# Placing the two operands of the split-precision matmuls 192 bytes apart modulo 512

## What is computed

```python
# layer 0
h = modulate(layernorm(x), shift_msa, scale_msa)
x = x + gate_msa * attention(h)              # 16 heads of 16 features, masked
h = modulate(layernorm(x), shift_mlp, scale_mlp)
x = x + gate_mlp * (gelu(h @ fc1.T + b1) @ fc2.T + b2)      # 256 -> 1024 -> 256
# layer 1
h = layernorm(x) * g + b + shift
q, k, v = split(h @ Wqkv.T)                  # 16 heads of 64 features, q and k normalized
x = x + (softmax(q @ k.T / 8) @ v) @ Wout.T
gate = softmax(x @ Wgate.T)                  # 8 experts, each takes its 1,024 best tokens
y = gelu(layernorm(tokens) @ fc1s[e].T + b1s[e]) @ fc2s[e].T + b2s[e]
x[tokens] += gate_value * y
```

## Time and profile before

| | us |
|---|---|
| median of three runs | 2468.11 |
| the profiled execution | 2465.28 |
| its span, first to last instruction | 2463.5 |
| TensorE busy with matmuls | 2333.9 (95%) |
| TensorE weight loads | 2072.9 (84%) |
| VectorE, ScalarE, GpSimd busy | 1908.8 (77%), 1549.2 (63%), 1030.6 (42%) |
| mean granted TensorE clock | 0.969 |

### The profile page before, as it was taken

One profiled execution on the slowest core, in us unless ns is written; L12 is line 12 of the kernel. 1 busy time (PEld: TensorE's weight loads), 2 busy tenths in 40 slices (PEclk: granted clock), 3 DMA queues, 4 the chain that ended last, 5 costly groups with the idle time before them and its releaser, 6 DMA issues. The chain is left out here.

```text
span 2463.5 us, 67114 instructions
## 1 busy us (share of the span) xinstructions
PE 2333.9 (95%) x24912; PEld 2072.9 (84%) x24912; DVE 1908.8 (77%) x3763; ACT 1549.2 (63%) x2982; POOL 1030.6 (42%) x939
## 2 busy tenths in 40 slices
PE   7999999999999899999999999999999727999997
PEld 6888888899999788888888888888888626999996
DVE  8999999667666688888888888888888586666663
ACT  6999998766666456565555656565555454556553
POOL 5888888200000234444343434344343203454543
PEclk9999999999999899999999999999999856999998
DMA  4111110101101000000000000000000112333422
GB/s 144 44 40 41 43 38 25 55 22 32 30 23 32 27 19 13 17 13 17 13 17 13 17 17 13 17 13 17 13 17 13 59 20 66 96 91 82 98 50 34
DMA packets 78720, 89.21 MB, mean 36 GB/s; under 512 B 18480, under 2 KB 72496, under 8 KB 76080
## 3 DMA queue, kind: packets, MB, share of 16 engines
q1 hardware_dynamic: 66352, 71.10, 9.3%
q0 software_dynamic: 12288, 17.05, 4.2%
HBM read 62.42 MB, written 25.69 MB: 36 GB/s over the span
## 5 line engine op out<-in xcount | busy, mean ns | idle before, releaser
L1275 POOL TENSOR_TENSOR a_rq<-a_vq,minus_half 128x8 f32<-128x8 f32 x256 | 417.4, 1640 | 97.9 <-DVE a_vq L1299 97.9
L1222 ACT ACTIVATE a_sq<-a_bqk 128x512 f32<-128x512 f32 x256 | 152.8, 597 | 351.0 <-PE a_bqk L126 348.5
L1270 POOL TENSOR_TENSOR a_rstd<-a_veps,minus_half 128x1 f32<-128x1 f32 x63 | 34.8, 552 | 580.5 <-DVE a_veps L1346 580.5
L124 PE MATMUL a_bqk<-wqk_hi,a_h_lo 128*128 128x512 f32 x512 | 207.4, 405 | 3.5 <-DVE a_h_lo L1315 3.5
L126 PE MATMUL a_bqk<-wqk_hi,a_h_hi 128*128 128x512 f32 x512 | 201.1, 393 | 0.0
L125 PE MATMUL a_bqk<-wqk_lo,a_h_hi 128*128 128x512 f32 x512 | 201.0, 393 | 0.0
L1291 DVE TENSOR_TENSOR a_qk<-a_bqk,a_rq 128x512 f32<-128x512 f32 x256 | 175.6, 686 | 29.8 <-POOL a_rq L1275 29.7
L2041 DVE TENSOR_TENSOR e_u_lo<-e_u,e_u_hi 128x512 fp32r<-128x512 f32 x128 | 88.8, 694 | 127.3 <-ACT e_u_hi L1904 126.6
L1899 ACT ACTIVATE e_u<-e_bu,e_b 128x512 f32<-128x512 f32 x128 | 88.3, 690 | 157.2 <-PE e_bu L126 155.2
L1207 ACT COPY a_vs<-a_ba 64x512 f32<-64x512 f32 x256 | 148.6, 580 | 53.6 <-PE a_ba L126 48.9
L1283 DVE TENSOR_REDUCE a_ss<-a_sq 128x8 f32<-128x512 f32 x256 | 173.7, 678 | 2.6 <-ACT a_sq L1222 1.0
(11 more groups left out here) (329 smaller groups left out, 8045.6 us busy)
## 6 DMA issues: line engine op xcount, KB each, us to landing
a_qk<-gates_of_rows SPq DMA_DIRECT2D x32, 256.0 KB, 4.3
tokens<-a_xs SPq DMA_DIRECT2D x64, 128.0 KB, 1.7
out<-a_xs SPq DMA_DIRECT2D x64, 128.0 KB, 1.7
e_w<-in_fc1s SPq DMA_DIRECT2D x8, 1024.0 KB, 4.9
e_w<-in_fc2s SPq DMA_DIRECT2D x8, 1024.0 KB, 4.9
a_gate<-gates_of_rows SPq DMA_DIRECT2D x122, 64.0 KB, 2.5
X<-in_x SPq DMA_DIRECT2D x56, 128.0 KB, 2.1
wst<-in_qkv_w SPq DMA_DIRECT2D x16, 128.0 KB, 2.5
```

What stands on the lines that cost most here:

```text
L124: tensor.matmul(to, w_lo, x_hi, start=start, stop=False)
L1222: nc.scalar.activation(sq[:, n * BK:(n + 1) * BK], b_qk[:, n * BK:(n + 1) * BK], ACT.Square).then_inc(s["sq"], 1)
L1275: nc.gpsimd.tensor_tensor(rq[:, 8 * n:8 * n + 8], vq[:, 8 * n:8 * n + 8], g.mhalf[:, 0:8], ALU.pow).then_inc(s["rq"], 1)
```

## The change

No instruction is added, removed or moved. The room of one small area changes, two groups of tensors change their order, and five unused tensors (a bare call of `m.sb`) fill gaps. 

```diff
-        small = m.sb("m0_small", [P, P])
+        small = m.sb("m0_small", [P, 64])          # MlpStart: 512 -> 256 bytes
...
-        st = m.sb("a0_st", [P, 6])                 # attention0_phase: these six tensors
-        veps = m.sb("a0_veps", [P, 1])             # move from ahead of a0_hT
-        mv = [m.sb(f"a0_mv{q}", [P, 2]) for q in range(2)]
-        rstd = [m.sb(f"a0_rstd{q}", [P, 1]) for q in range(2)]
         hT = m.sb("a0_hT", [P, DC, T2])
...
         o_hi, o_lo = (m.sb("a0_o_" + n, [P, DC, P], F32R) for n in ("hi", "lo"))
+        st = m.sb("a0_st", [P, 6])
+        veps = m.sb("a0_veps", [P, 1])
+        mv = [m.sb(f"a0_mv{q}", [P, 2]) for q in range(2)]
+        rstd = [m.sb(f"a0_rstd{q}", [P, 1]) for q in range(2)]
         wp_hi, wp_lo = (m.sb("a0_wp_" + n, [P, DC, D], F32R) for n in ("hi", "lo"))
...
+        m.sb("m0_apart", [P, 48])                  # mlp0_phase, ahead of its tensors
         b2 = m.sb("m0_b2", [P, D])
...
+        m.sb("e_ahead", [P, 56])                   # experts_phase
         w1_hi, w1_lo = ([m.sb(f"e_w1_{n}{q}", [P, DC, MLP], F32R) for q in range(2)] for n in ("hi", "lo"))
         w2_hi, w2_lo = ([m.sb(f"e_w2_{n}{q}", [P, MC, D], F32R) for q in range(2)] for n in ("hi", "lo"))
         uf = m.sb("e_u", [P, RING, GTOK])
+        m.sb("e_apart", [P, 80])
         u_hi, u_lo = (m.sb("e_u_" + n, [P, RING, GTOK], F32R) for n in ("hi", "lo"))
...
+            g.mlp = MlpStart(m0)                   # program
+            m0.sb("pair_apart", [P, 16])
             g.pair_hi, g.pair_lo = (m0.sb("pair_" + n, [P, DC * GTOK], F32R) for n in ("hi", "lo"))
-            g.mlp = MlpStart(m0)
+            m0.sb("tokens_apart", [P, 48])
             g.X = m0.sb("X", [P, NT, D])
```

More of the change, by code:

```diff
@@ L174, in __init__ @@
     def __init__(self, m):
-        small = m.sb("m0_small", [P, P])
+        small = m.sb("m0_small", [P, 64])
         self.b1 = small[:, 0:MC]
[L177 to L180, removed]
+        self.st = small[:, 8:8 + 6 * GT].rearrange("p (k n) -> p k n", k=GT)
+        self.mv = small[:, 32:32 + 2 * GT].rearrange("p (k n) -> p k n", k=GT)
+        self.veps = small[:, 40:40 + GT]
+        self.rstd = small[:, 48:48 + GT]
         self.s = {n: m.sem("m0_" + n) for n in self.NAMES}
```

## The result

Six runs of the changed kernel took 2447.45 us in the median (2446.81 to 2448.41), six of the kernel before 2467.38 us (2464.95 to 2471.71). The ratio is 0.9916, with a 95% interval of 0.9906 to 0.9926: the change makes the kernel 19.9 us faster. The prediction had a gain of 13.6 us and 2454.5 us. The profiled execution took 2448.41 us, its span is 2446.6 us (2463.5 before).

A forecast was written before the change was run, and what follows sets the result against it. TensorE was taken to bound MLP and experts, with VectorE having little room in the first attention. 10.1 + 2.6 + 0.9 = 13.6 us off 2465.28 gave 2451.7 us, as a median 2454.5 us; range 2441 to 2469 us.

The forecast's parts named there:

- The distance sets the pace: Split matmuls: operand distance modulo 512 decides the time per matmul, 13.6 us gained in all; forecast's chance 0.54.
- The rival that order alone does it: Split products: order, not distance, sets the pace, so nothing changes: 2468 us, give or take 3; chance 0.16.
- The `down` side: Experts' and MLP's `down`, first attention's v and output: 3,840 matmuls at +192 fall to 116.9 ns, gaining 10.1 us.
- The quick pace's rival: All split products go quick, 114.5 ns at +192: 28.9 us, cut by VectorE to 26.0, giving 2442 us; chance 0.14.
- The `up` side: Experts' and MLP's `up`: 1,536 matmuls of 512 columns at -192 fall from 231.2 to 229.5 ns, gaining 2.6 us.
- q and k: First attention: 768 matmuls of 256 columns at -192, half of a 1.8 us gain taken, 0.9 us.
- The bad mirror distance: Distance -192 in `up`, q and k slows them, losing 8.7 us net: 2477 us; chance 0.07.
- Moved float32 products: First attention's product of probabilities and v, moved from distance -192 to 0: costed at nothing, 3 us if its cover fails.
- VectorE's cover: First attention: VectorE's elastic L543 gives at least 67 ns a tile, 4.3 us, so the 2.7 us gain fits.

The follow-up runs named there:

- run 1: Changed kernel without the 320 bytes of padding ahead of e_u_hi, so all split operands of the experts lie at distance 0: 2454.13 us.
- run 2: Changed kernel with the experts' `up` back at distance 0 (`down` stays +192) and the MLP's `down` back at 0 (`up` stays -192): 2459.95 us.
- run 7: Changed kernel with the experts' `up` at distance 256 instead of -192, `down` left at +192: 2454.53 us.
- run 10: Changed kernel, experts: `up` at -128 in the first half of an expert's tokens and -64 in the second, `down` at +192: 2451.13 us.
- run 12: Changed kernel with the experts' `down` at -64 and `up` at +64: median 2448.90 us, ratio 0.9928 to the kernel before.
- run 3: Changed kernel with experts' `down` at -192 and `up` at +192, MLP's `down` at +256 and its odd groups' `up` at -256: 2463.74 us.
- run 8: Changed kernel with the second attention's h moved by 64 bytes, its q, k and v from distance +256 to +192: 2454.97 us.
- run 6: Changed kernel with experts' `down` at +224 and `up` at -224, MLP's `down` at +160 and its odd groups' `up` at -160: 2463.60 us.
- run 4: Changed kernel with only the low part of the experts' u at distance 0 from w2, the high part staying at +192: 2456.36 us.

## Why the prediction was right, and what it mis-sized

**The distance sets the pace: right.** The rival that order alone does it (2468 us) fell in run 1: same order, only the distance taken back, 8.0 us lost. But what comes before a product decides as well, and that is the part that the forecast left open.

**The `down` side, 10.1 us: mis-sized.** That each nanosecond of a matmul shortens these stages was right, and so was the count; the pace that the sum went by was too slow. In the MLP and the experts it gave 1.440 - 1.387 = 0.053 us and 1.433 - 1.386 = 0.047 us in each of 128 runs: 6.8 + 6.0 = 12.8 us, where the sum had 4.8 + 3.5 = 8.3. The price was 116.9 ns, the mean of two paces in the second attention's output; measured are 115.5 ns. The caution that "the way in which a run is entered decides between them, and I can't tell it for the new order" was right: in the new order every run is entered from an `up` at -192, falls at the sixth matmul into the quick pace (113.3 ns) and stays there. Runs 2 and 7 show that the entry does it: with `down` at +192 all the same, but `up` at 0 or 256, it keeps 117.7 ns, close to the forecast's price, and the experts gain 2.8 us instead of 8.1. In the first attention, whose output and v come in runs of six, 12 went from 119.2 to 116.7 ns, 1.9 us, and the price was right (1.8), as the mean of a quicker output and a slower v. The quick pace's rival had 114.5 ns for all, 28.9 us; its pace came about in 7 of 12 matmuls. The 12.8 us lie nearer to that rival's 15.7 for these two stages (1,536 x 4.7 + 1,536 x 5.5) than to the 8.3 of the sum, and 2447.45 us nearer to its 2442 than to the forecast's 2454.5: the measured time is at the lower edge of what the forecast called its own (2447 to 2462).

**The `up` side, 2.6 us: right in kind, a little small.** 1.389 to 1.374 us in the experts and 1.388 to 1.375 in the MLP are 1.9 + 1.7 = 3.6 us; 229.5 ns was forecast and 229.0 measured. No row had shown the distance, so that the size was a guess between two bounds and its hit is luck. That this term can be added to the other is a coincidence of this pair of distances: by run 2, `up` at -192 beside a `down` at 0 is 233.8 ns, slower than before, and by runs 10 and 12 what is best for `down` (`up` at -64 modulo 512) isn't best for `up`.

**q and k, 0.9 us: right.** 119.5 to 117.9 ns behind the first gap, which grew from 199 to 202 ns: a run of 12 is 14 ns shorter, 64 x 14 = 0.9 us. **The bad mirror distance** shows on the other side: 512 columns at +192 take 233.6 ns (run 3) and 233.2 (run 8), at -192 229.0. It isn't a property of the distance alone: beside a `down` at +192 an `up` at -64, the same modulo 256 as +192, takes 231.4 (run 10), and beside a `down` at 0 an `up` at -192 takes 233.8 (run 2). 256 columns at -192 take 117.6 to 117.9, in the middle.

**Moved float32 products at nothing: right.** The 32 products of probabilities and v of a tile (L732) take 1057 ns in the median before and after, and the first attention got shorter by what its split products gave. **VectorE's cover: right.** The tiles came 47 ns closer (ten tiles in 64.07 us before, in 63.60 after: 3.0 us over 64 tiles, 2.7 forecast), and L543 went down by 48 ns, within the 67 ns that it had.

**Sum.** By lengths of runs 6.0 + 6.8 + 1.9 + 1.9 + 1.7 + 0.9 = 19.2 us, beside 19.9 us between the medians. The two profiled executions lie 16.9 us apart: of the first attention's 3.0 us the MLP's start shows 1.7 (it lies between 447.0 and 451.2 us in the runs above whose first attention is the same, so that it is no measure of tenths), and the MLP began at a granted clock of 0.75 in its first 4 us, where before it was 1.00; in runs whose MLP began at full clock it took 366.9 us, 8.2 less than before. By stages the forecast had -5.2, -5.8 and -2.7 us; measured were -8.1, -7.3 and about -3.

## What to carry to other kernels

Where TensorE is the bound and its matmuls stream 256 or 512 columns of fp32r, look at the places of the two operands modulo 256 bytes: in `down` the moving operand 192 bytes ahead of the stationary one, in `up` 192 behind it, gave 0.8% here for a few bytes of padding. Measure whole loops, not a product alone: the product before helps to decide which pace the next one finds. One side alone gave 2.8 us in the experts, where both gave 8.1, and cost 1.6 us in the MLP, where both gave 7.3. Price such a change by the distances between starts, matmul by matmul, and look whether a run settles in a pace, rather than by a mean over runs that were entered in different ways.

## What the hardware showed that was not expected

- With distances on a grid of 64 bytes a long run of equal matmuls mostly settles in one of a few paces: for 256 columns 113.3, 117.7 or 120 ns, for 512 columns 226.7 (second attention's v), about 229 or 233.5 ns. The quick pace isn't entered at once: after an `up` at -192 it takes one slip of 123 ns at the fourth matmul. In run 6, off the grid, the starts go on changing (121, 117, 118, 117, 122, 116, 116, 120 ns and so on).
- The distance counts modulo 256 bytes: 0 as 256 (`down` 1.433 and 1.435 us), -192 as +64 (1.411 both), +128 as -128 (`up` 1.388 and 1.389), +192 as -64 (`down` 1.386 both). Distances off the grid of 64 bytes lie between (1.417 and 1.419).
- The best pair found is `down` (256 columns) at +192 with `up` (512 columns) at -192; the weights are 128 columns wide in both. Of the three distances of `down` beside which `up` stood at -192 or +64 (192, 64 and 0), only 192 let it gain. Whether it is the width that makes the two differ was not tested.
- What exactly meets at a bad distance, the stream with the load of its own weights or of the next, stays open: run 4 was meant to tell, and its pace changed in all three matmuls at once. No kernel here beat the change.
